# Attention on one Trainium2 core: tiles 8 to 12 of a batch scored in a row, the next batch's remaining values behind them

## The reference

```python
Q = (x_q @ W_Q + b_Q).reshape(B, L, H, dk).transpose(0, 2, 1, 3)      # x_q: layernorm(x), H = 16, dk = 16
K = (x_k @ W_K + b_K).reshape(B, S, H, dk).transpose(0, 2, 1, 3)      # x_k = x_v: the context, S = 1601
V = (x_v @ W_V + b_V).reshape(B, S, H, dk).transpose(0, 2, 1, 3)
scores = jnp.einsum('bhld,bhsd->bhls', Q, K) / jnp.sqrt(jnp.float32(dk))
attn = jax.nn.softmax(scores, axis=-1)
ctx = jnp.einsum('bhls,bhsd->bhld', attn, V)
```

## Time and profile before

| | |
|---|---|
| median of 3 runs | 2298.77 us (2298.0 to 2299.25) |
| the profiled execution | 2295.68 us, span 2294.0 us |
| granted TensorE clock, mean | 0.967 |
| TensorE matmuls busy | 2110.6 us (92%) |
| TensorE weight loads busy | 1741.3 us (76%) |
| VectorE busy | 1426.7 us (62%) |
| ScalarE busy | 1241.0 us (54%) |
| POOL busy | 764.7 us (33%) |

### The profile page before, as it was taken

One profiled execution on the slowest core, in us unless ns is written; L12 is line 12 of the kernel. 1 busy time (PEld: TensorE's weight loads), 2 busy tenths in 40 slices (PEclk: granted clock), 3 DMA queues, 4 the chain that ended last, 5 costly groups with the idle time before them and its releaser, 6 DMA issues. The chain is left out here.

```text
span 2294.0 us, 65086 instructions
## 1 busy us (share of the span) xinstructions
PE 2110.6 (92%) x28676; PEld 1741.3 (76%) x28676; DVE 1426.7 (62%) x2619; ACT 1241.0 (54%) x1680; POOL 764.7 (33%) x571
## 2 busy tenths in 40 slices
PE   6999999999999999999999999789599997699993
PEld 4888889999999999999988988644132337599993
DVE  4655555555555555555555554446788875688885
ACT  2355555555555555555555554258799981365551
POOL 2223222222222222222222220000799962265551
PEclk8999999999999999999999999899899998799997
DMA  3111111111111111111111110214874531666663
GB/s 100 38 47 42 40 48 42 40 48 42 40 48 43 40 48 42 40 48 42 40 48 43 40 41 7 66 48 145 239 176 138 146 84 44 222 216 210 218 230 124
DMA packets 131138, 195.41 MB, mean 85 GB/s; under 512 B 18116, under 2 KB 109252, under 8 KB 130696
## 3 DMA queue, kind: packets, MB, share of 16 engines
q1 hardware_dynamic: 121832, 174.98, 25.4%
q0 software_dynamic: 4416, 12.06, 1.6%
q10 hardware_dynamic: 4608, 4.20, 0.5%
HBM read 159.61 MB, written 31.59 MB: 83 GB/s over the span
## 5 line engine op out<-in xcount | busy, mean ns | idle before, releaser
L543 DVE TENSOR_REDUCE max_part<-work 128x1 f32<-128x384 f32 (+1 forms) x1024 | 534.8, 569 | 179.7 <-PE work L671 156.3
L606 ACT ACTIVATE probs<-scores 128x1024 f32<-128x1024 f32 (+1 forms) x416 | 423.6, 1026 | 333.1 <-PE scores L696 321.8
L497 POOL TENSOR_TENSOR ctx_lo<-ctx_whole,ctx_hi 128x768 fp32r<-128x768 f32 (+1 forms) x128 | 231.2, 1807 | 1025.3 <-DVE ctx_hi L526 1013.6
L538 DVE SCALAR_TENSOR_TENSOR keys_lo<-work,bk,keys_hi 128x384 fp32r<-128x384 f32 (+1 forms) x256 | 162.5, 635 | 329.3 <-ACT keys_hi L585 329.3
L1307 POOL TENSOR_TENSOR decay<-steps_in,xn 128x1024 f32<-128x1024 f32 x126 | 243.7, 1970 | 132.3 <-POOLq L915 115.0
L690 PE MATMUL scores<-q_hi,keys_hi 64*128 64x256 f32 (+1 forms) x1664 | 253.2, 283 | 2.0 <-issue 1.3
L690 PE MATMUL scores<-q_hi,keys_lo 64*128 64x256 f32 (+1 forms) x1664 | 249.2, 278 | 1.1 <-issue 1.0
L690 PE MATMUL scores<-q_lo,keys_hi 64*128 64x256 f32 (+1 forms) x1664 | 249.0, 277 | 0.7 <-issue 0.7
L661 PE MATMUL work<-wv_hi,ctx_hi 128*128 128x256 f32 (+1 forms) x832 | 244.3, 294 | 0.2
L661 PE MATMUL work<-wv_hi,ctx_lo 128*128 128x256 f32 (+1 forms) x832 | 234.6, 282 | 0.0
L661 PE MATMUL work<-wv_lo,ctx_hi 128*128 128x256 f32 (+1 forms) x832 | 234.4, 282 | 0.0
(11 more groups left out here) (233 smaller groups left out, 4604.2 us busy)
## 6 DMA issues: line engine op xcount, KB each, us to landing
xs<-in_w_T SPq DMA_DIRECT2D x46, 1024.0 KB, 7.8
ctx_whole<-in_ctx_T SPq DMA_DIRECT2D x96, 384.0 KB, 3.3
steps_in<-scratch_results SPq DMA_DIRECT2D x256, 128.0 KB, 2.7
ctx_whole<-in_ctx_T SPq DMA_DIRECT2D x32, 449.0 KB, 3.4
scratch_results<-steps SPq DMA_DIRECT2D x16, 512.0 KB, 2.6
scratch_mixed<-mixed ACTq DMA_DIRECT2D x32, 128.0 KB, 3.2
scratch_z<-z SPq DMA_DIRECT2D x16, 256.0 KB, 3.7
zg<-scratch_z SPq DMA_DIRECT2D x16, 256.0 KB, 3.4
```

Source lines behind the costliest of these rows:

```text
L497: nc.gpsimd.tensor_tensor(ctx_lo[c][:, :, 0:n], s.ctx_whole[c % 2][:, :, 0:n], ctx_hi[c][:, :, 0:n].bitcast(F32), ALU.subtract).then_inc(l ...
L538: nc.vector.scalar_tensor_tensor(keys_lo[par][:, m, start:start + n], bank[:, 0:n], s.bk[:, m:m + 1], keys_hi[par][:, m, start:start + n]. ...
L543: nc.vector.reduce_max(max_part[par][:, place(pair), c:c + 1], bank[:, 0:CHUNKS[c][1]], AX) \
L606: nc.scalar.activation(probs[n % PROBS][0:rows, :], scores[slot][0:rows, :], ACT.Exp, scale=1.0 / HD ** 0.5).then_inc(exp_done, 1)
```

## The change

Three entries of the order become one. Before: tiles 8 and 9 with two maxima ahead of each, behind them two maxima and the values of tiles 6, 7 and 8; tiles 10 and 11 with two maxima ahead of each, behind them two maxima and the values of tiles 9 and 10; tile 12 with the last two maxima ahead of it, and the values of tiles 11 and 12 and the row behind it. After: tiles 8 to 12 with two maxima ahead of each, then the last four maxima, the values of tiles 6 to 12, and the row. Number and kinds of units are the same.

```diff
     ([6, 7], [maxima(1, 4, 6), maxima(1, 6, 8)],
      maxima(2, 0, 2) + keys_unit(0, 3) + keys_unit(1, 3) + values_unit(5)),
-    ([8, 9], [maxima(2, 2, 4), maxima(2, 4, 6)],
-     maxima(2, 6, 8) + values_unit(6, 7) + values_unit(8)),
-    ([10, 11], [maxima(3, 0, 2), maxima(3, 2, 4)],
-     maxima(3, 4, 6) + values_unit(9, 10)),
-    ([12], [maxima(3, 6, 8)],
-     values_unit(11, 12) + [("row",)]),
+    ([8, 9, 10, 11, 12], [maxima(2, 2, 4), maxima(2, 4, 6), maxima(2, 6, 8), maxima(3, 0, 2), maxima(3, 2, 4)],
+     maxima(3, 4, 8) + values_unit(6, 7) + values_unit(8) + values_unit(9, 10) + values_unit(11, 12) + [("row",)]),
 ]
```

## The result

The changed kernel takes 2311.56 us in the median (2308.61 to 2315.07, 4 runs), before it is 2298.69 us (2298.0 to 2299.25, 4 runs). The ratio is 1.0053, with a 95% interval from 1.0039 to 1.0067: slower by 12.9 us. The forecast was 4 us slower, on the edge of what can be measured, with 2317 as the upper end. The direction came out and the time lies in the range, but most of the loss has another cause than the one worked out.

What follows compares the result with a forecast made beforehand. TensorE, busy 92% of the span, was taken to bound the kernel. 31 batches at 0.17 us give 5.3, less 1.1 in batch 0's preparation: +4.2 us, predicted 2303.0 us, range 2293 to 2317.

Steps and rivals of the forecast that it cites:

- The part rebuilt from its spacings: Loop batch from first maxima ahead of tile 8 to row: 12.55 us instead of 12.38, 0.17 later per batch.
- gate of the exp: Tiles 10 and 12 wait until the exp two tiles earlier has read its bank: 0.09 and 0.03 us.
- the single one that I described: One TensorE wait per batch, 1.2 us, ahead of the values, until the sixth pair's second reduce frees its bank.
- The preparation of batch 0: Fourteen maxima in a row, then values partly at slow clock: row at 82.3 instead of 83.42, a gain of 1.1 us.
- I cost all this at nothing: Later release of chunk 2, with its cast, subtraction and the load of next batch's chunk 0: no cost.
- The cover that I named: Chunk 0's load is wanted over 10 us later and lands in 3.3; without cover, 1.8 us per batch.
- The clock did not fall in the loop: Rival: 1.2 us idle per batch lowers TensorE's clock for 16 matmuls; +48 us, 2350; chance 0.06.
- any clock below 1.00 in the loop: Sign of being wrong: TensorE's granted clock under full anywhere in the loop; full clock was expected.
- The gate of ScalarE: Rival in the scores of tiles 8 to 12: maxima do not fill the exp waits; 2316 us or little under; chance 0.12.
- The burst was not free: Rival: the last four maxima do not hold the values; 0.9 us per batch faster, 2272; chance 0.12 with its halves.
- the gate in full: Exp waits between scores paid whole, 0.46 us as upper bound; 2316 us or a little under; chance 0.12.
- the slower side was the likelier: Chances for the whole kernel: slower 0.48, no change 0.42, faster 0.10.

Runs made afterwards that it cites:

- after_short: The changed kernel with the reduces of the last four maxima (last chunk) over 64 columns instead of 449; 2289.15 us, 0.9957 of before.
- split: The changed kernel with two of the last four maxima moved behind the values of tiles 6 to 8; 0.9983 of before.
- after_c0_late: The changed kernel with the load of a batch's chunk 0 held until the mix of tiles 8 to 12 is through; 2300.05 us, 1.0001 of before.
- before_c0_mix: The kernel before with the load of chunk 0 held until all units ahead of the row are made, so it moves during the mix; 2307.19 us, 1.0033.
- after_shift: The changed kernel with 128 already met waits added to TensorE's program ahead of the preparation of batch 0; 1.0061 of before.

## Why the prediction was right or wrong

*The part rebuilt from its spacings* was right to 0.05 us: gate of the exp 0.09 at tile 10 (that at tile 12, 0.03, did not show), places of all pairs, values at 7.47 (7.52), row at 12.52 (12.55). Per batch it gave 0.17 and the trace has 0.15. The waits of this part were not the single one that I described, but three that sum up to it. after_short shows that the reduces hold the values, split that fewer in one go cost less.

*The preparation of batch 0* gained 1.8 where I had 1.1, inside its bounds. The clock stood at its 1.2 GHz level from 72 to 78 us, through the burst, and was back at 2.4 GHz with 30 of the 42 values matmuls still to come, where I had 26.

*"I cost all this at nothing"* is the step that failed. I followed the load of chunk 0 to the one who waits for it, found 10 us of slack, and stopped. The load is never late, and still it costs some 8 us (after_c0_late, before_c0_mix), since its bytes pass the DMA engines just when TensorE's program needs its next packet, in the longest stretch of short instructions of the batch (320 in 2.4 us). The packet comes later by that, TensorE stands idle for longer, and in two batches the clock falls behind it. The cover that I named hid the load's own latency and nothing of what the load takes from others. The trace of before had the signs, which I did not read: row-to-key stretches of 4.75 in the middle and 6 us in the first batches, and TensorE's idle times put down to issue there. I priced the loop from a batch in its middle, which has none.

*The rivals.* The clock did not fall in the loop on account of the burst: it is 1.00 in the middle batches with 1.1 us of waits each. It did fall twice behind the long idle times of batches 1 and 3, some 3 us in all, and "any clock below 1.00 in the loop" was one of my own signs of being wrong. What brought it down was the wait for instructions, which no rival had. The Trainium skill's warning of short idle times while banks are cycled (TensorE: Matmul & The Clock Gate, A second HAM failure mode) did not come true for waits of this length: three of 0.35 to 0.43 us per batch. The gate of ScalarE was not paid in full. The burst was not free. The time of 2311.56 lies where "the gate in full" would have put it, for another reason: the two traces, not the time, tell the two apart. That the slower side was the likelier was right for the part that I had worked out: it gave +4.2, and these two terms measured +4.7 and -1.8, so 2.9 of the 12.9 us. That the whole lies inside the range is luck, since the upper bound came from a gate that was not paid.

## What to carry to other kernels

A load that is moved has two prices: when it lands, and what else wants the DMA engines while it moves; the fetch of the next instructions is among the latter, and here it showed as idle time that no semaphore ended. Where a loop's batches differ, price the change in more than one of them. And units that share a ring of banks and are slow to evacuate are better spread than made in one go ahead of other work: here two goes of two maxima beat one of four by 0.41 us per batch, though the second costs one more change of kind.

## What the runs showed of the hardware

TensorE stood still up to 2.5 us at a time for a packet of 16 KB of its own program, and its next instruction came 2.2 to 2.8 us after the packet moved. A load over all DMA engines in the same 2 us made the packet move later, in the batch shown 2.4 instead of 1.6 us behind the row; put there alone it cost 7.9 us of 2299. Which batches are hit hangs on where the program's packets end: 64 more instructions moved the idle times from batches 1 to 9 and 27 to 30 to batches 6 to 16 and left their sum at 19 us. Behind single idle times of 2.17 and 2.29 us (1.61 once in after_shift) the granted clock fell to its 1.2 GHz level; behind one of 1.94 it did not; with three waits of 0.35 to 0.43 us per batch it stayed at full in the middle batches.
